# Attention of a slot under the streams, a searched order for stage A, and a fused AND/OR

## The reference

```python
n = layernorm(x)
q = n @ Wq + bq                                   # 16 heads of 64
summary[c] = mean of n over the 64 rows that end at row 64*c
k, v = summary @ Wk + bk, summary @ Wv + bv       # 128 chunks
s = q k^T / 8, masked to chunks whose end is <= the row
x = x + softmax(s) v @ Wo + bo
m = layernorm(x)
h = gelu(blockquant(m) @ blockquant(w_fc)^T)      # 1024 -> 4096
x = x + blockquant(h) @ blockquant(w_proj)^T      # 4096 -> 1024
```

## Time and profile before

| what | us |
|---|---|
| median of 3 runs (lowest, highest) | 920.89 (919.87, 923.05) |
| profiled execution | 924.51 |
| its span on the slowest core (3) | 922.9 |
| spans of the other cores | 912.7 to 918.5 |
| busy over the span: PE, DVE, ACT | 752.9, 682.4, 405.8 |

### The profile page before, as it was taken

One profiled execution on the slowest core, in us unless ns is written; L12 is line 12 of the kernel. 1 busy time (PEld: TensorE's weight loads), 2 busy tenths in 40 slices (PEclk: granted clock), 3 DMA queues, 4 the chain that ended last, 5 costly groups with the idle time before them and its releaser, 6 DMA issues.

```text
span 922.9 us, 13778 instructions; the slowest of 8 cores (912.7 to 922.9 us)
## 1 busy us (share of the span) xinstructions
PE 752.9 (82%) x4598; PEld 419.5 (45%) x4598; DVE 682.4 (74%) x1069; ACT 405.8 (44%) x655; POOL 81.6 (9%) x129
## 2 busy tenths in 40 slices
PE   0146596583878878857895999999999999999998
PEld 0012232230523323212564678668485675847645
DVE  1686877687679989875568599979779596895751
ACT  2466887764266746545544234325051340603200
POOL 3021221000000010001000000000010000001010
PEclk9997897785566978777998999999999999999999
DMA  8999999999865556536686022314041240313032
GB/s 206 239 244 246 228 236 219 190 233 253 169 203 179 197 199 221 190 96 177 220 259 183 24 47 47 70 23 86 7 69 47 30 86 2 68 23 46 2 77 61
DMA packets 60453, 124.62 MB, mean 135 GB/s; under 512 B 22488, under 2 KB 29024, under 8 KB 56288
## 3 DMA queue, kind: packets, MB, share of 16 engines
q0 software_dynamic: 22384, 54.80, 30.1%
q1 hardware_dynamic: 38000, 68.94, 24.1%
HBM read 112.45 MB, written 25.17 MB: 149 GB/s over the span
## 4 chain that ended last, share of the span: by engine, by line
PE 58%; DVE 14%; DMA 12%; issue 7%; ACT 7%; SPq 1%; DVEq 0%; ACTq 0%; POOL 0%; POOLq 0%
PE psX L1183 11%; PE psY L1183 11%; PE psOT L1137 10%; PE psS L1137 6%; DMA xs<-xoth 6%; PE psV L1137 6%; PE psOT L910 3%; DVE wfcT L457 2%; PE psY L709 2%; DMA wst<-wfc_in 2%; DMA wpT<-wpq_scr 2%; DVE nmf L834 2%; SPq L153 1%; DMA wst<-wpj_in 1%; DMA xt<-y 1%
## 5 line engine op out<-in xcount | busy, mean ns | idle before, releaser
L1183 PE MATMUL psX<-wpT,hq 128*128 128x512 bf16 x448 | 134.9, 383 | 7.1 <-DMA wpT<-wpq_scr 5.9
L1183 PE MATMUL psY<-wpT,hq 128*128 128x512 bf16 x448 | 134.6, 382 | 0.0
L1141 ACT ACTIVATE h<-psV,bfc 128x256 f32<-128x256 f32 x64 | 30.3, 474 | 199.8 <-PE psV L1137 183.5
L1148 DVE TENSOR_REDUCE hpart<-h 128x256 f32<-128x1024 f32 x56 | 107.9, 1927 | 13.0 <-ACT h L1141 13.0
L1137 PE MATMUL psOT<-xqT,wfcT 128*128 128x256 bf16 x896 | 107.1, 273 | 0.5 <-ACT h L1141 0.5
L709 PE MATMUL psY<-lnT,WA 128*128 128x512 bf16 x256 | 70.2, 426 | 42.9 <-ACT lnT L337 18.9
L1137 PEld LDWEIGHTS psOT<-xqT,wfcT 128*128 128x128 bf16 x896 | 87.6, 98 | 10.9 <-issue 0.8
L1170 DVE TENSOR_TENSOR hq<-h,hM 128x1024 bf16<-128x1024 f32 x64 | 78.0, 1219 | 1.0 <-DVE hM L1161 0.2
L1183 PEld LDWEIGHTS psX<-wpT,hq 128*128 128x128 bf16 x448 | 44.1, 98 | 59.7 <-issue 9.3
L1137 PE MATMUL psV<-xqT,wfcT 128*128 128x256 bf16 x512 | 66.4, 273 | 4.6 <-DVE oTa L1005 2.4
L1141 ACT ACTIVATE h<-psOT,bfc 128x256 f32<-128x256 f32 x112 | 52.9, 473 | 37.8 <-PE psOT L1137 37.8
(11 more groups left out here) (157 smaller groups left out, 1211.3 us busy)
## 6 DMA issues: line engine op xcount, KB each, us to landing
wst<-wfc_in SPq DMA_DIRECT2D x16, 1024.0 KB, 7.0
wst<-wpj_in SPq DMA_DIRECT2D x16, 1024.0 KB, 10.1
xr<-xown POOLq DMA_DIRECT2D x31, 512.0 KB, 8.3
xs<-xoth POOLq DMA_DIRECT2D x24, 512.0 KB, 14.8
wpq_scr<-uq SPq DMA_DIRECT2D x16, 512.0 KB, 10.2
xt<-y SPq DMA_DIRECT2D x16, 512.0 KB, 3.9
wpT<-wpq_scr SPq DMA_DIRECT2D x16, 512.0 KB, 7.3
y<-xr POOLq DMA_DIRECT2D x15, 512.0 KB, 4.3
```

Source lines behind the costliest of these rows:

```text
L1141: fbank_free[b] = op("scalar", lambda E, e=e, ps=ps: E.activation(out=h[:, e, :], in_=ps, func=ACT.Gelu, bias=bfc[:, e:e + 1]), after=[tk, ...
L1148: tr_ = op("vector", lambda E, c=c, dst=dst: E.tensor_reduce(out=dst, in_=h[:, 4 * c:4 * c + 4, :].rearrange("p e t -> p t e"), axis=AXX, ...
L1183: return op("tensor", lambda E: E.matmul(ps.rearrange("p (c n) -> p c n", n=64), hq[r][:, e % 4, 128 * u:128 * u + 128], wpT[:, 8 * hf:8 * ...
```

## The change

1. **A slot's attention starts once its own chunk sums are complete.** With 6 stream steps per slot, the sums of slot s are complete after step 6s+5. Centring, turning, `kT`, `vv` and the row maxima are done per slot on 32 rows (`c_prep`), four times in place of once. Own tiles now come two per stream step, in steps 0 to 7, so that all queries are there early. Wq and Wk are asked for at the start, Wv after the last query.
2. **Stage A as chains.** Each part is a generator (20 of them, one letter each) with its own conditions, and a string of 809 letters, found by a search, says which chain takes the next step. It replaces the hand-written loops. Of the string one line stands below.
3. **The projection of the last slot moves into stage A**, ahead of the first fc1. A projection step evicts 1024 columns at once in place of 512, alternating between `psOT` and `psX`, and the residual tiles have 4 buffers.
4. **AND and OR in one operation.** Keeping the exponent and multiplying by 24 become one: with magnitudes scaled by 16 at no cost in ScalarE's pass, (bits AND 0x7F80) OR 0x0040 is 1.5 times the power of two. The floor moves into the last level of the tree, which becomes a scalar_tensor_tensor. The variance of a stream step takes 2 small operations in place of 3.
5. The `wpT` loads are asked for over tiles 0 to 22 of the first fc1, and wait for the last projection and the last writes of residual tiles. The weight staging stays at 3 buffers.

```diff
+ORDER = (
+    "aabbaacdbeabvcfvomadefgobhffmohbhcohgaqrqabqrravaqbdmrqerqffaboacrqmudehaoqmrbffbcoahhohrgqqumbaarde"
...
+def take_turns(chains):
+    for c in ORDER:
+        assert next(chains[c], False), c
...
-            t = op("vector", lambda E: E.tensor_scalar(
-                out=pw.bitcast(U16), in0=pw.bitcast(U16),
-                scalar1=0x7F80, scalar2=None, op0=ALU.bitwise_and), after=[t])
-            t = op("vector", lambda E: E.tensor_scalar(
-                out=mm, in0=pw, scalar1=24.0, scalar2=float(24.0 * 2.0 ** -126),
-                op0=ALU.mult, op1=ALU.max), after=[t, trm_free[n % 2]])
+                t = op("vector", lambda E, mm=mm, pw=pw: E.tensor_scalar(
+                    out=mm.bitcast(U16), in0=pw.bitcast(U16), scalar1=0x7F80, scalar2=0x0040,
+                    op0=ALU.bitwise_and, op1=ALU.bitwise_or), after=[t, trm_free[n % 2]])
...
+        def c_prep():
...
+            for s in range(NSLOT):
+                while s not in ready:
+                    yield False
+                R = slice(32 * s, 32 * s + 32)
+                t = op("vector", lambda E, R=R: E.tensor_reduce(out=smn[R, 0:1], in_=psX[R, :], axis=AXX, op=ALU.add),
+                       after=[ready[s]])
...
+                for m in range(8):
+                    for j in range(8):
+                        tk = op("tensor", lambda E, m=m, j=j, R=R: E.matmul(
+                            psT[:, 32 * m:32 * m + 32], WB[:, j, 128 * m:128 * m + 128], summT[:, j, R],
...
+        def c_project():
...
+            for t in range(16):
+                s, u, k = t // 4, t % 4, t % 4
+                while done["l"] < 8 * (s + 1) or t not in xa_tok or NSLOT - 1 not in t_v:
+                    yield False
...
                 if g == 0:
-                    for i in range(8):
-                        hook(1 + 3 * i, lambda i=i: (squares(), o_unit(3, i)))
-                    hook(25, squares)
-                    for c in range(12):
-                        hook(2 * c, lambda c=c: load_wp(c, wp_after[c] + [gelu_tok[max(0, 2 * c - 2)]]))
+                    for c in range(16):
+                        hook(c + c // 2, lambda c=c: load_wp(c, wp_after + [gelu_tok[c + c // 2]]))
```

More of the change, by code:

```diff
@@ L362, in build_nc @@
+        jobs += [("fc", i) for i in range(7, 16)]
+        done = {"i": 0, "j": 0}
         job = {}
-        n_pj = {"i": 0}
-        n_fc = {"i": 0}
+        pj_before = [sum(j[0] == "pj" for j in jobs[:n]) for n in range(len(jobs))]
+        fc_before = [sum(j[0] == "fc" for j in jobs[:n]) for n in range(len(jobs))]
+        wpq_tok = {}
+        wfc_tok = {}
         def load_job(n):
+            if n >= len(jobs):
+                return
             kind, i = jobs[n]
             k = n % 3
-            if k == 2 and st["late"]:
-                k = 3
@@ L505, in build_nc, with top @@
-        bg = weights()
-        bg_state = {"done": False}
-        def background(steps):
-            for _ in range(steps):
-                if bg_state["done"]:
-                    return
-                try:
-                    next(bg)
-                except StopIteration:
-                    bg_state["done"] = True
+        def top(v, lo, t):
+            return op("vector", lambda E: E.scalar_tensor_tensor(
+                out=v[:, 0:lo], in0=v[:, 0:lo], scalar=float(2.0 ** -122), in1=v[:, lo:2 * lo],
+                op0=ALU.max, op1=ALU.max), after=[t])
@@ L568, in build_nc @@
         lnT_tok = {}
+        own_tok = {}
         qps_free = [None, None]
+        q_tok = {}
         qT_tok = {}
@@ L767, in build_nc @@
-        assert not q_todo and not q_owed and t_wv is not None
-        t_S = S_last["tok"]
-        st["stream_end"] = [t_S, gat_free[0], gat_free[1]]
-        while any(k == 2 and (n, "end") not in job for n, (k, _) in wload.items()):
-            background(1)
-        t = op("vector", lambda E: E.tensor_reduce(out=smn[:, 0:1], in_=psX, axis=AXX, op=ALU.add), after=[t_S])
-        t = op("vector", lambda E: E.tensor_scalar(out=smn[:, 1:2], in0=smn[:, 0:1], scalar1=-1.0 / D,
-                                                   scalar2=None, op0=ALU.mult), after=[t])
@@ new lines, in c_var @@
+        def c_var():
+            for k in range(NSTEP):
+                while done["b"] <= k:
+                    yield False
+                kk = k % 2
+                a = acs[kk]
+                t = op("vector", lambda E, a=a: E.scalar_tensor_tensor(
+                    out=a[:, 2:3], in0=a[:, 0:1], scalar=-1.0 / D ** 2, in1=a[:, 0:1], op0=ALU.mult, op1=ALU.mult),
+                    after=[sums[(k, 0)]])
+                sums[(k, 2)] = op("vector", lambda E, a=a, kk=kk: E.scalar_tensor_tensor(
+                    out=mva[kk][:, 1, 1:2], in0=a[:, 1:2], scalar=1.0 / D, in1=a[:, 2:3], op0=ALU.mult, op1=ALU.add),
+                    after=[t, sums[(k, 1)]] + mva_free[kk])
+                done["c"] = k + 1
+                yield True
@@ new lines, in c_qdrain @@
+        def c_qdrain():
+            for n in range(32):
+                s, m = n // 8, n % 8
+                while done["q"] <= n:
+                    yield False
+                ps = psY[:, 512 * (m % 2):512 * (m % 2) + 512]
+                qT_tok[s] = qps_free[m % 2] = op("scalar", lambda E, m=m, ps=ps, s=s: E.activation(
+                    out=qT[:, m, 512 * s:512 * s + 512], in_=ps, func=ACT.Identity,
+                    bias=bqr[:, m:m + 1]), after=[q_tok[n], t_bias])
+                done["r"] = n + 1
+                yield True
@@ L939, in squares, with c_square @@
+        def c_square():
+            for t in range(16):
+                k = t % 4
+                while t not in nm2_tok or (t == 0 and done["b"] < NSTEP):
+                    yield False
+                tq = op("scalar", lambda E, k=k, t=t: E.activation(
+                    out=junk[0], in_=xa_buf[k], func=ACT.Square, bias=nm2[:, t:t + 1],
+                    accum_out=ssq[:, t:t + 1]), after=[nm2_tok[t], sq_prev["tok"] or sums[(NSTEP - 1, 0)]])
                 sq_prev["tok"] = tq
                 xa_free[k] = [xm_tok[t], tq]
-                n = 15 if t == 12 else t + 2
@@ new lines, in c_norm2 @@
+        def c_norm2():
+            while 0 not in ab2_tok or done["b"] < NSTEP or done["x"] < 24:
+                yield False
+            xt_free[0] = sums[(NSTEP - 1, 1)]
+            xq_free[0] = []
+            xq_free[2] = [sel_free[0]]
+            xqT_free[0] = xr_free[3][0]
+            for u in range(2):
+                x2_load(0, u)
+                yield True
+                x2_norm(0, u)
+                yield True
+                x2_quant(0, u)
+                x2_turn(0, u)
+                yield True
```

1104 lines of the change are left out of this document (534 added, 570 removed).

## The result

| | before | after |
|---|---|---|
| median, us (3 runs before, 4 after) | 920.89 | 906.19 |
| ratio (95% interval) | | 0.9838 (0.9814 to 0.9862) |
| profiled execution, us | 924.51 | 905.73 |
| its span on the slowest core | 922.9 (core 3) | 904.2 (core 6) |
| A: to the first fc1 matmul | 443.5 | 442.0 (forecast 417) |

A forecast was written before the change was run, and what follows sets the result against it. VectorE's work at its achievable density was taken to bound the time up to fc1, with transfers limiting the streams: 417 + 40 + 419.1 + 1.6 outside the span = 877.7, less 3.6, gives 874 us; range 856 to 905.

The forecast's parts named there:

- A: Stretch up to the first fc1 matmul, 443.5 us before: forecast 417, ends 396 and 441.
- B: From the first fc1 matmul to the first fc2 matmul that runs on, 60.3 us before: forecast 40, ends 38 and 52.
- C: Rest of the span, from 503.8 us on before: untouched by the change, so it stays at 419.1 us.
- the offset: The median of the runs lies 3.6 us below the profiled execution; taking that off turns 877.7 into 874 us.
- The work of VectorE in A: VectorE's busy time before fc1: 329.7 us becomes 329, of which 322 must be done before fc1 can start.
- Which density: VectorE's busy share from 50 us to fc1: 0.82 assumed, between bounds 0.77 (stream phase) and 0.87 (258.5 to 410 us).
- the hole: 228 to 258.5 us before, sums turned into keys and values, VectorE at 0.66: claimed to go with the change.
- The first 50 us: Start-up at the kernel's beginning: 21.2 us of VectorE work, claimed to stay as before.
- The streams' end: Last stream matmul: 248 us used, from 246 by VectorE's work and 241 by transfers alone; past 265 would show it wrong.
- Rival 3: Streams slip, with late `xs` buffers and idle transfer engines: streams end at 259, total 887 or 899; chance 0.10.
- Rival 1: TensorE becomes the bound behind the streams: 195 us there, 443 up to fc1, total 900; chance 0.17.
- Rival 4: A slot's preparation stays exposed and holds the streams: slower than before, total 931 at 60% of 95 us; chance 0.08.

## Why the prediction was wrong

The direction was right, the size not. By its own sum: A +25.0, B +6.1, C -3.0 and the offset +4.1 (the profiled execution was 0.5 below the median this time, not 3.6 above) make 874 into 906.2.

- *The work of VectorE in A*, 322 us: 322.07. The edits inside that were looked at were sized well too: the fused operation takes 227 and 182 ns, a residual addition of 1024 columns 1219, a centring on 32 rows 1219, as on 128. The last tree levels as scalar_tensor_tensor take 425 and 225 ns (292 and 192 before), +2.7 us where I took +3:

```profile
L417 DVE SCALAR_TENSOR_TENSOR gat<-gat 128x256 bf16<-128x256 bf16 x15 | 6.4, 425 | 1.6
...
L417 DVE SCALAR_TENSOR_TENSOR uq<-uq 128x64 bf16<-128x64 bf16 x16 | 3.6, 225 | 2.0 <-DVE uq L412 0.5
```

- *"Which density"* is the step that failed: 0.82 for all of A behind the first 50 us. I took the mean over 50 to 410 us (0.80) and left out the thin end, 410 to 443.5, although A was the quotient up to fc1; over all of it the kernel before shows 0.784. And I counted the hole as gain, with transfers as a reason only for stopping short of 0.87. The 0.82 came true behind the streams (0.824 in 174.2 us, where I had 169) and failed under them (0.758): of the 25 us by which A is longer than forecast, 20 lie ahead of the last stream matmul. With transfers light, the same order gives 0.831 and 414.9 us, close to my 0.82 and 417; with transfers at full size it gives 0.787 and 442. So what transfers cost in this order, 27 to 31 us, was not priced. The rows that said so were there: a share of 0.97 and 1.01 up to 228 us, with VectorE at 0.77.
- *"The first 50 us are start-up, 21.2 us of work, and stay."* They did not: 13.55. The change asks for all of Wq, 4 MB, at 6 to 11 us among the first rows on one queue (Wk follows from 42.6 us on). The kernel before asked for two pieces of Wq at a time. I followed the chains of that move but not the queue: own tile 4, asked for at 31 us, lands behind Wq. Of the 7.6 us lost, 3.5 came back without Wq's volume.
- *The streams' end*, 248: 267.8, past the 265 that I had set as a sign of being wrong. With light transfers 250.9. Neither bound taken alone gives that: the work up to there is 178.6 us where I had 182, and the windows' rates make 53.2 MB of transfers, 232 us at the 229 GB/s of before. By 200 us, with transfers at 0.95 or more, VectorE had done 118.6 us of work, where the kernel before had done 137.3; from there on transfers are at 0.57, and VectorE, at 0.885, is what holds the streams. Rival 3 had this sign and, at its 0.77, 259; its mechanism (buffers that come free late, transfer engines idle) is not what the share of 0.95 up to 200 us shows, and with 887 to 899 it fell short too.
- *B*, 40: 46.1. I priced the `wpT` loads by their bytes and did not ask what stands behind them on SP's queue: the transpose of group 1, 9.77 us. Without that, 40.7 and 39.7, so the 38 to 40 of the working holds as a number; it still ends in a wait for `xqT`, though, and not for `wpT` as I had it.
- *C* came 3.0 us shorter, 413.38 us of TensorE's time where it was 416.00, at a clock of 1.00 and 0.99. Nothing was run on it, and its cause is open.
- *TensorE.* Rival 1 named 900 us and an A of 443, near the time measured, but that is luck: it had streams until 248 and 195 us behind them, and the trace has 267.8 and 174.2. Between 267.8 and 385 us TensorE was busy 0.75 at clock 0.78. The key matmuls were mis-sized as well: I took the stationary side for their cost, 100 ns each and +19 us. The row shows 7.4 us for all 256, 29 ns each:

```profile
L807 PE MATMUL psOT<-summT,WB 128*128 128x32 bf16 x256 | 7.4, 185 | 4.1 <-DVE summT L801 2.9 <-DVE acs L609 1.2
```

  The four groups take about the same time at either level of the clock. Two windows around such a group of 64, at a granted clock of 1.00 and of 0.50:

```profile
158.10:160.50 2.40, 1.91 (x66) 1.68 (x64) 0.70 (x2) 2.31 (x4) 0.90 (x1) 1.00 0.98 318
...
273.50:275.40 1.90, 1.87 (x66) 1.86 (x68) 1.90 (x3) 1.90 (x2) 0.00 (x0) 0.50 0.58 134
```

  By the rule I had cited from the Trainium skill, "TensorE: Matmul & The Clock Gate", section on LDWEIGHTS, they would take 27 us; the trace doesn't bear that out. The same page's section "Weight-path perf modes" says that weights of 128 columns that aren't fp32 are loaded in four parallel chunks, with a gain of 4 in theory, for fp8, and of about 2 as measured. By its figures a load would be 27 ns at a gain of 4 and 53 ns at 2, both estimates. The trace's 27 to 29 ns fit the first and not the second, and I had stopped one section short. Whether the load is what sets them isn't shown: at the lower clock 32 moving columns could as well, being a quarter of the 100 ns that 128 took in the earlier trace rows; at the full clock they could not. TensorE wasn't the bound, so no term of the sum changes.
- *Rival 4* (a preparation that holds the streams) did not happen, and the first scores come at 186 us, before 200 as expected. Up to 267.8 us the longest wait of TensorE in the preparation lines is 5.8 us, for Wv, and the next 4.5, for VectorE; the whole loss of VectorE to transfers is several times that.

## What to carry to other kernels

- When a stage runs with its transfer engines full, closing a hole on a compute engine can merely move the idle time to the waits for transfers (here 14 us left the stretch behind the streams and 20 came up under them), unless bytes go too. Work that has been taken in from another stage (here the projections) is then the gain, and not a shorter stage.
- One density for a whole stage hides two limits: take it for each phase, and count what a phase that waits for transfers can do apart from one that waits for nothing but its own engine.
- Take a density over exactly the stretch whose length is computed from it, and follow each issuing queue as an engine of its own: what is asked for earlier makes what stands behind it later, on GpSimd's queue (Wq before rows) as on SP's (`wpT` before a transpose).
- To learn what transfers cost, shrink their volume and keep the order; shifting parts of a searched order tests the order instead.

## What the runs showed of the hardware

- 64 matmuls with 128 stationary and 32 moving columns run in 1.75 to 1.87 us, 27 to 29 ns each, at a granted clock of 1.00 and of 0.50; in the earlier trace rows 64 with 128 moving columns took 6.4 us, at a mean granted clock of 0.56. The record of one weight load lasts 95 to 109 ns all the same, so the loads overlap.
- Asked for at 6 to 11 us, among and behind loads of rows on one queue, the eight pieces of Wq took 34.6 us (median) to land, at a transfer share of 0.98. The kernel before asked for them two at a time between 7 and 56 us, and they took 15.5.
- A scalar_tensor_tensor on two bf16 inputs costs 425 ns at 256 columns where tensor_tensor costs 292, and 225 against 192 at 64.
- A tensor_reduce over 1024 columns of PSUM takes 1219 ns on 32 rows and 1225 ns on 128.
